# Query norm of a gated-delta attention phase: row sums by one-column matmuls of the squares instead of four transposes and squares with accumulation

## The reference, cut to what matters

```python
q, k, v = silu(conv(mixed))                      # q, k: 16 heads x 128, v: 32 heads x 128
q = inv_scale ** 2 * _rms_norm(q)                # x * rsqrt(mean(x*x) + 1e-6)
k = inv_scale * _rms_norm(k)
# a scan over tokens: state decays, delta = (v - k.state) * beta, state += k x delta, o = q.state
xn = _rms_norm(out) * norm_w
gated = silu(z) * xn
return gated @ W_out
```

## Time and profile before

| | |
|---|---|
| median of 3 runs | 3748.02 us (3746.4 to 3748.84) |
| the profiled execution | 3746.4 us, its span in the trace 3744.6 us |
| TensorE (PE) busy | 3522.7 us, 94% of the span |
| GpSimd (POOL) busy | 2233.1 us, 60% |
| VectorE (DVE) busy | 2110.6 us, 56% |
| ScalarE (ACT) busy | 2081.8 us, 56% |
| granted TensorE clock, mean | 0.976 |

### The profile page before, as it was taken

The page is one execution under the profiler, slowest core; times in us unless marked ns, Lnnn a source line. Parts: engine busy times, 40 slices in busy tenths (PEclk is TensorE's granted clock), DMA queues, the critical chain, the costliest instruction groups (busy, mean ns, idle before and its releaser), DMA issues. The chain is left out here.

```text
span 3744.6 us, 76942 instructions
## 1 busy us (share of the span) xinstructions
PE 3522.7 (94%) x29092; PEld 2941.4 (79%) x29092; DVE 2110.6 (56%) x4091; ACT 2081.8 (56%) x5616; POOL 2233.1 (60%) x2645
## 2 busy tenths in 40 slices
PE   5996599999999999999999999999999999996898
PEld 3884388888888888888888888888888888885787
DVE  4654355555555555555555555555555555552564
ACT  3442266666666666666666666666666666663343
POOL 2101467676767676767676767677777777762110
PEclk8998799999999999999999999999999999997999
DMA  4314112121212121212121212121212121210421
GB/s 152 116 35 83 61 53 74 64 74 64 74 64 74 64 74 64 74 64 75 68 76 64 75 66 80 67 75 64 78 66 80 63 75 67 71 57 35 163 57 35
DMA packets 207871, 270.34 MB, mean 72 GB/s; under 512 B 86160, under 2 KB 117264, under 8 KB 206352
## 3 DMA queue, kind: packets, MB, share of 16 engines
q1 hardware_dynamic: 202464, 250.02, 20.4%
q0 software_dynamic: 4464, 14.36, 1.0%
q10 hardware_dynamic: 576, 1.03, 0.1%
HBM read 176.05 MB, written 89.13 MB: 71 GB/s over the span
## 5 line engine op out<-in xcount | busy, mean ns | idle before, releaser
L1892 ACT ACTIVATE at_t<-at_inv 128x512 f16<-128x512 f32 x768 | 460.2, 599 | 509.2 <-PE at_inv L1701 509.2
L1480 PE MATMUL at_proj<-x_hi,at_w_hi 128*128 128x512 f32 x1024 | 437.6, 427 | 18.0 <-POOL at_w_lo L2151 18.0
L1480 PE MATMUL at_proj<-x_hi,at_w_lo 128*128 128x512 f32 x1024 | 421.5, 412 | 0.0
L1480 PE MATMUL at_proj<-x_lo,at_w_hi 128*128 128x512 f32 x1024 | 415.6, 406 | 0.0
L2230 POOL TENSOR_TENSOR at_gt_lo<-at_cst,at_gates 128x512 fp32r<-128x512 f32 x256 | 261.9, 1044 | 250.2 <-PE at_misc L1480 250.2
L2077 DVE TENSOR_TENSOR at_pml<-at_prod,at_cst 128x256 f16<-128x256 f32 x768 | 322.8, 420 | 147.4 <-PE at_prod L1480 136.5
L2047 DVE TENSOR_TENSOR at_rows<-at_misc,at_rows 128x512 f32<-128x512 f32 x256 | 177.0, 692 | 282.3 <-PE at_misc L1480 281.7
L1480 PE MATMUL at_prod<-at_t,at_nlhi 128*128 128x64 f16 (+1 forms) x3584 | 287.3, 197 | 24.7 <-ACT at_t L1890 13.3
L1480 PE MATMUL at_proj<-at_w_hi,x_hi 128*128 128x256 f32 x1024 | 308.5, 301 | 0.8 <-DVE at_cv_q L2002 0.8
L1480 PE MATMUL at_proj<-at_w_hi,x_lo 128*128 128x256 f32 x1024 | 308.0, 301 | 0.0
L1480 PE MATMUL at_proj<-at_w_lo,x_hi 128*128 128x256 f32 x1024 | 302.3, 295 | 0.0
(11 more groups left out here) (290 smaller groups left out, 10631.3 us busy)
## 6 DMA issues: line engine op xcount, KB each, us to landing
at_rows<-x SPq DMA_DIRECT2D x64, 1024.0 KB, 5.6
x<-at_rows SPq DMA_DIRECT2D x64, 1024.0 KB, 4.2
at_gb<-decays SPq DMA_DIRECT2D x64, 512.0 KB, 3.7
at_raw<-w_qkvz SPq DMA_DIRECT2D x46, 512.0 KB, 3.6
ffn_weights<-ffn_w SPq DMA_DIRECT2D x1, 11776.0 KB, 36.8
ffn_w<-ffn_weights POOLq DMA_DIRECT2D x4, 2688.0 KB, 23.3
at_raw<-w_out SPq DMA_DIRECT2D x16, 512.0 KB, 3.5
f_xnext<-x_in SPq DMA_DIRECT2D x4, 1024.0 KB, 5.2
```

The lines of the kernel that those rows point to most:

```text
L1480: return nc.tensor.matmul(out, lhsT, rhs, start=start, stop=stop)
L1892: own["a_t"].up(A(grown(t16[:, s % R].rearrange("p a t -> p (a t)"), s // R), grown(psT[s % R], s // R), ACT.Copy))
```

## The change

The row sums of the squared q are no longer taken from a transposed q. ScalarE squares the 128x512 `cv_q` in one instruction into `sq[:, 1]`, in step 14 of the first half of the slot. TensorE multiplies each 128x128 chunk of it, as the stationary operand, with one column of ones, which leaves 4 columns of sums in the bank `psT[0]` (`sums`, in `fill[15]`). VectorE scales them and adds epsilon (128x4). GpSimd makes the q factor and its square of it with 3 small instructions. The second norm now multiplies by that square, adds its epsilon, takes the power and multiplies by the q factor: 4 chained instructions in `out_scale` instead of 3. `turn_q` is gone. The projections V0, V1 and K are dealt out anew over `fill[15]` and the gaps; their number stays. TensorE waits for VectorE's read of the sums (`d_ss`) before `turn_v(0)`, which writes the same bank. The waits for `a_sq` in `high`, `kq_of` and `out_scale` go.

```diff
@@ pe_pass
-                def turn_q():
-                    wait(pe, "p_silu", 3 * j + 2)
-                    wait(pe, "a_ex", R * (j + 1))
-                    for c in range(CH):
-                        last = nc.tensor.transpose(ch(psM, c), ch(cv_q, c), ident)
-                    own["s_qtr"].up(last)
+                def sums():
+                    wait(pe, "a_sq", j + 1)
+                    wait(pe, "d_ss", j)
+                    for c in range(CH):
+                        last = mm(psS[:, c:c + 1], ch(sq[:, 1], c), ones[:, 0:1])
+                    own["s_ss"].up(last)
...
-                    fill[15].append(parts(V0_U, 4, 12))
-                    gap[0].append(parts(V1_U, 0, 3))
+                    fill[15] += [parts(V0_U, 4, 9), sums]
+                    gap[0].append(parts(V0_U, 9, 12))
...
-                    gap[5] += [turn_q, parts(V1_U, 8, 10)]
-                    gap[6].append(parts(V1_U, 10, 12))
+                    gap[5].append(parts(V1_U, 5, 9))
+                    gap[6].append(parts(V1_U, 9, 12))
...
-                        gap[9].append(parts(K_U, 8, 12, j + 1))
+                        gap[9].append(parts(K_U, 7, 12, j + 1))
...
                     turn_kn()
+                    wait(pe, "d_ss", j + 1)
@@ act_pass
                 def square_q():
-                    wait(act, "s_qtr", j + 1)
-                    wait(act, "p_fr", j)
-                    for c in range(CH):
-                        last = A(ch(squared, c), ch(psM, c), ACT.Square, scale=(0.25 * Q_EPS / D) ** 0.5, accum_out=qe[:, nxt, c:c + 1])
-                    own["a_sq"].up(last)
+                    wait(act, "p_silu", 3 * j + 2)
+                    wait(act, "s_ss", j)
+                    own["a_sq"].up(A(sq[:, 1, :], conv_out(Q_U), ACT.Square))
...
                     steps[12].append(square_k)
+                    steps[14].append(square_q)
...
                             tanh(V0_U)
-                            square_q()
@@ dve_pass
+                def sums():
+                    wait(dve, "s_ss", j + 1)
+                    wait(dve, "p_rk", 2 * j)
+                    own["d_ss"].up(V.tensor_scalar(ss[:, CH:2 * CH], psS, 0.25 / D, EPS_RMS, ALU.mult, ALU.add))
...
+                if has_prep:
+                    sums()
                 if has_delta:
                     silu_z(Z1_U)
@@ pool_pass, out_scale
-                    chain(G.tensor_tensor(sso[:], sso[:], qe[:, of % 2, :].unsqueeze(1).to_broadcast([P, R, CH]), ALU.add))
-                    chain(G.tensor_scalar(flat, flat, Q_EPS * EPS_RMS, None, ALU.add))
-                    own["p_fr"].up(G.tensor_tensor(fr[:].rearrange("p h c -> p (h c)"), flat, half[:], ALU.pow))
+                    chain(G.tensor_tensor(sso[:], sso[:], qs2[:, of % 2, :].unsqueeze(1).to_broadcast([P, R, CH]), ALU.mult))
+                    chain(G.tensor_scalar(flat, flat, 4 * EPS_RMS, None, ALU.add))
+                    chain(G.tensor_tensor(flat, flat, half[:], ALU.pow))
+                    own["p_fr"].up(G.tensor_tensor(fr[:], sso[:], scale[:, of % 2, CH:2 * CH].unsqueeze(1).to_broadcast([P, R, CH]), ALU.mult))
@@ pool_pass, after mask_g(0)
+                    wait(pool, "d_ss", j + 1)
+                    chain(G.tensor_tensor(rr[:, CH:2 * CH], ss[:, CH:2 * CH], half[:, CH:2 * CH], ALU.pow))
+                    chain(G.tensor_tensor(scale[:, nxt, CH:2 * CH], rr[:, CH:2 * CH], cst[:, C_KSC + CH:C_LATER], ALU.mult))
+                    own["p_rk"].up(G.tensor_tensor(qs2[:, nxt, :], scale[:, nxt, CH:2 * CH], scale[:, nxt, CH:2 * CH], ALU.mult))
```

More of the change, by code:

```diff
@@ L48 @@
 SEGS, WINS = 6, 16
-C_ID, C_INCL, C_KSC = (i * P for i in range(3))
-C_LATER = C_KSC + CH
+C_ID, C_ONES, C_INCL, C_KSC = (i * P for i in range(4))
+C_LATER = C_KSC + 2 * CH
 C_END = C_LATER + P
@@ L285, in constants @@
     c[:, C_LATER:C_LATER + P] = row > col
+    c[:, C_ONES:C_ONES + P] = 1
     c[:, C_INCL:C_INCL + P] = row <= col
     c[:, C_KSC:C_KSC + CH] = INV / 2
+    c[:, C_KSC + CH:C_LATER] = INV * INV / 4
     h = np.zeros((P, C16_END), np.float16)
@@ L1257 @@
 UNITS = NK * B
-Q_EPS = 64 * D * D * EPS_RMS
 def attn_phase(nc, w_qkvz, conv_w, norm_w, w_out, cst_in, cst16_in, x_dram, x_hi, x_lo, gate_dram, decay_dram, y_dram):
@@ L1277, in attn_phase @@
         cst16 = sb("cst16", [P, C16_END], F16)
-        ident, incl = (cst[:, a:a + P] for a in (C_ID, C_INCL))
+        ident, ones, incl = (cst[:, a:a + P] for a in (C_ID, C_ONES, C_INCL))
         ident16, two16 = (cst16[:, a:a + P] for a in (0, C16_TWO))
@@ L1296, in attn_phase @@
         sq = sb("sq", [P, 2, S])
[L1297 to L1300, removed]
+        ss = sb("ss", [P, 2 * CH])
+        rr = sb("rr", [P, 2 * CH])
+        scale = sb("scale", [P, 2, 2 * CH])
+        qs2 = sb("qs2", [P, 2, CH])
         kn = sb("kn", [P, CH, D])
@@ L1321, in attn_phase @@
         ks = sb("ks", [P, R, CH - 1, D])
-        squared = nlhi[:].rearrange("p r s -> p (r s)").bitcast(F32)
         flat = t16[:].rearrange("p r a t -> p (r a t)").bitcast(F32)
@@ L1343, in attn_phase @@
         psO = [psT[1][:, 512:1024], psP[:]]
+        psS = psT[0][:, 768:768 + CH]
         unit_bank = [psA[i] for i in (0, 1, 0, 1, 0, 1)]
@@ L1349, in attn_phase @@
         names = ["l_taps", "l_wo", "l_gates", "l_gb", "l_kq", "l_v", "l_z", "l_x",
-                 "s_proj", "s_z", "s_qtr", "s_ktr", "s_dg", "s_g", "s_kq", "s_p", "s_t", "s_e", "s_t1", "s_v", "s_y", "s_u", "s_o", "s_gtr", "s_w",
+                 "s_proj", "s_z", "s_ss", "s_ktr", "s_dg", "s_g", "s_kq", "s_p", "s_t", "s_e", "s_t1", "s_v", "s_y", "s_u", "s_o", "s_gtr", "s_w",
                  "a_tap", "a_th", "a_thz", "a_ssk", "a_sq", "a_kn", "a_knT", "a_ex", "a_hi", "a_t", "a_t1", "a_v", "a_d", "a_sqo", "a_gt",
-                 "d_conv", "d_silu", "d_z", "d_nl", "d_aqk", "d_p", "d_e", "d_s", "d_gate", "d_lo", "d_y", "d_link",
+                 "d_conv", "d_silu", "d_z", "d_ss", "d_nl", "d_aqk", "d_p", "d_e", "d_s", "d_gate", "d_lo", "d_y", "d_link",
                  "p_w", "p_wo", "p_z", "p_gt", "p_silu", "p_gm", "p_ex", "p_diag", "p_t0", "p_lo", "p_dcy", "p_kg", "p_qg", "p_ks", "p_rk", "p_fr", "p_link"]
         sems = {n: sem(n) for n in names}
-        AHEAD = {"s_proj": 4, "s_qtr": 1, "s_ktr": 2, "s_dg": R, "a_tap": 4, "a_th": 4, "a_ssk": 1, "a_sq": 1, "a_kn": 1, "a_knT": 1, "a_ex": R,
-                 "d_conv": 4, "d_silu": 1, "p_silu": 3, "p_gm": R, "p_ex": R, "p_rk": 1}
+        AHEAD = {"s_proj": 4, "s_ss": 1, "s_ktr": 2, "s_dg": R, "a_tap": 4, "a_th": 4, "a_ssk": 1, "a_sq": 1, "a_kn": 1, "a_knT": 1, "a_ex": R,
+                 "d_conv": 4, "d_silu": 1, "d_ss": 1, "p_silu": 3, "p_gm": R, "p_ex": R, "p_rk": 2}
         def slots():
@@ L1607, in kq_of @@
                 def kq_of(i):
-                    wait(pe, "a_sq", i)
+                    wait(pe, "a_ex", R * i)
                     wait(pe, "p_silu", 3 * i - 1)
@@ L1662, in pe_pass @@
                     fill[14].append(parts(V0_U, 0, 4))
-                    fill[15].append(parts(V0_U, 4, 12))
-                    gap[0].append(parts(V1_U, 0, 3))
+                    fill[15] += [parts(V0_U, 4, 9), sums]
+                    gap[0].append(parts(V0_U, 9, 12))
                     gap[1].append(lambda: gram_of(j + 1))
                     gap[2].append(lambda: decay(0))
-                    gap[3].append(parts(V1_U, 3, 7))
-                    gap[4] += [lambda: decay(1), parts(V1_U, 7, 8)]
-                    gap[5] += [turn_q, parts(V1_U, 8, 10)]
-                    gap[6].append(parts(V1_U, 10, 12))
+                    gap[3].append(parts(V1_U, 0, 4))
+                    gap[4] += [lambda: decay(1), parts(V1_U, 4, 5)]
+                    gap[5].append(parts(V1_U, 5, 9))
+                    gap[6].append(parts(V1_U, 9, 12))
                     gap[10] += [lambda: level_0(j + 1, 0), lambda: kq_of(j + 1)]
                     if j + 2 < UNITS:
-                        gap[6].append(parts(K_U, 0, 2, j + 1))
-                        gap[7].append(parts(K_U, 2, 6, j + 1))
-                        gap[8].append(parts(K_U, 6, 8, j + 1))
-                        gap[9].append(parts(K_U, 8, 12, j + 1))
+                        gap[6].append(parts(K_U, 0, 1, j + 1))
+                        gap[7].append(parts(K_U, 1, 5, j + 1))
+                        gap[8].append(parts(K_U, 5, 7, j + 1))
+                        gap[9].append(parts(K_U, 7, 12, j + 1))
                 if not has_delta:
@@ L1842, in square_q @@
                 def square_q():
-                    wait(act, "s_qtr", j + 1)
-                    wait(act, "p_fr", j)
-                    for c in range(CH):
-                        last = A(ch(squared, c), ch(psM, c), ACT.Square, scale=(0.25 * Q_EPS / D) ** 0.5, accum_out=qe[:, nxt, c:c + 1])
-                    own["a_sq"].up(last)
+                    wait(act, "p_silu", 3 * j + 2)
+                    wait(act, "s_ss", j)
+                    own["a_sq"].up(A(sq[:, 1, :], conv_out(Q_U), ACT.Square))
```

(23 more changed lines are left out.)

## The result

The changed kernel takes 3776.95 us (median of 4 runs, 3776.14 to 3784.43) against 3748.05 us for the kernel before (median of 4 runs). The ratio of the runs is 1.0082 with an interval of 1.0066 to 1.0097: 29 us slower, where 37 were forecast, and inside the forecast range of 3760 to 3808 us. The profiled execution took 3779.27 us.

The account below looks back on a forecast made before the run. The prediction took TensorE's issue stream to bound the kernel. 64 x 0.40 = 25.6 us on TensorE and 63 x 0.18 = 11.3 us from GpSimd make 37 us, giving 3785 us, range 3760 to 3808.

Parts of the forecast that it names:

- What bounds the kernel: Attention phase: TensorE's issue stream sets the slot of 46.25 us; its time counts in full, ScalarE savings for nothing.
- What goes and what comes on TensorE: TensorE's slot: four q transposes (0.43 us) go, eight fp32 loads and one-column moves (0.83 us) come, +0.40 us.
- GpSimd: `out_scale`: the fourth chained instruction, 0.29 us against 0.11 us slack, makes `turn_gated(0)` 0.18 us late a slot.
- the third rival: Existing TensorE waits absorb part of the loss, or GpSimd's step is hidden: 3755 to 3774 us, chance 0.12.
- The new wait of TensorE: Before `turn_v(0)`: the wait for VectorE's read of the sums stays hidden, by 0.2 us.
- What is only moved: `fill[15]` and the gaps: the same 32 projection matmuls keep their time, and gaps covering waits hold at least as much.
- The first rival: `sums` in `fill[15]`: loads hide or are short, 0.03 us a record, giving 3736 or 3747 us; chance 0.11.
- What would show it: Changed kernel's profile: stretch 0.8 to 0.9 us, slot 46.8 us, `turn_gated` waiting some 0.2 us for GpSimd in nearly every slot.

Follow-up runs that it names:

- e2: The changed kernel with 64 columns of ones moved in each of the four sums instead of one; 3783.57 us.
- e3: The changed kernel with squares and ones column in fp16, 4 records with fp16 loads in place of 8 with fp32 loads; 3758.16 us.
- e9: The changed kernel with the dealing of before, fp16 squares, VectorE making the epsilon term and two chained GpSimd instructions in `out_scale`; 3726.73 us.
- e1: The changed kernel with GpSimd's `out_scale` back at three chained instructions (add, add, power) instead of four; 3772.66 us.
- e8: The changed kernel with two more chained 128x8 multiplications by one in `out_scale` on GpSimd; 3811.36 us.
- e6: The kernel before with only the new dealing of the V0, V1 and K projections, `turn_q` staying in `gap[5]`; 3778.63 us.

## Why the prediction was right, and where it was not

- *What bounds the kernel.* Right. What went into TensorE's stream was paid in full, and ScalarE's lighter load bought nothing.
- *What goes and what comes on TensorE.* Right. The one-column records take 0.81 us (0.83 forecast); with `turn_q`'s 0.43 us gone that is +0.38 a slot (+0.40 forecast), 24 of the 29 us. That it is the loads was shown from two sides: 64 columns cost 0.02 us more (e2), the same sums with fp16 loads take 0.12 us (e3, e9). By the Trainium skill ("TensorE: Matmul & The Clock Gate", LDWEIGHTS) a load takes its 128 columns over 1.2 GHz, 107 ns; an estimate from that is 8 loads less `turn_q`, 0.43 us a slot. The trace has 0.116 us between loads, one of them hidden.
- *GpSimd.* The mechanism is right, its size was off: 0.18 us a slot forecast, 0.11 to 0.12 measured (e1, e8 and the offsets). I took the delay of the first load of `turn_gated`, and that came as worked out, 0.17 us. But 0.05 us of it was slack: the four transposes with their loads took 0.54 us from the first load to the next matmul before (1860.31 to 1860.85) and 0.49 after (1832.85 to 1833.34). What holds up the stream is the matmul behind them, 0.12 us late. So the slack was 0.05 us larger than the 0.11 I gave. Over 63 slots this is 4 of the 8 us between 37 and 29. The waits that were there took up nothing (e8), so the third rival is not the reason.
- *The new wait of TensorE.* Right, 0.2 us of cover.
- *What is only moved.* The sum was right, the reason was not. I checked the gaps that gained matmuls and not the place that lost three. There `turn_kn` waits for ScalarE's k; in the kernel before, ScalarE was only some 0.3 us ahead of it. The sums, at 0.81 us, happen to fill the 0.70 us that left. That this term came out at nothing was luck: had they been cheap, the hole would have opened, as in e3.
- *The first rival's price.* Wrong for that reason. I said 3736 to 3747 us if each of the eight records cost 0.03 us, 0.24 us together. e3 has cheaper sums still, 0.12 us, and took 3758.16 us. With 0.24 us, `turn_kn` would have waited for k as well (newton(0), which starts at 1852.13 in the trace of the changed kernel, to `turn_kn` would be 2.48 - 0.81 + 0.24 = 1.91 us, under the 2.05 us that k takes), so e3's time is also the estimate for that case. A forecast of no change would have been 10 us off with the rival's own mechanism granted.
- *What would show it.* The slot and the stretch came as forecast. The row of a wait for GpSimd in every slot did not; it is there only with e8's longer delay.

Not tried: the sums in the reduced fp32 type of the projections, whose matmuls show as one record with one load each. What makes up the 4 us ahead of the first slot in the profiled execution stays open too; the slots explain 30 of 33.

## What to carry to other kernels

To sum over partitions with one column of ones, the data becomes the stationary operand, and its load is the price: here 0.116 us for each of the two records of a 128x128 block in fp32, with 1 column moved and nearly the same with 64, and 0.03 us a block in fp16. These squares only decide how much the second norm's epsilon weighs, so fp16 was open to them. When matmuls are moved on the engine that bounds, look at the place that they leave: what stood behind them had its wait hidden by them.

## What the runs showed that was not expected

Dealing 3 of 32 projection matmuls of a slot to other places cost 0.47 us a slot (e6), as much as a change with real work in it. PE's own row names only 0.26 us of it. The row of its weight loads names more, 0.43 us a slot (530 to 3400 us: total, times, longest):

```profile
PE at_misc L1586 <- ACT at_kn L1862: 16.1, 62, 0.3
PEld at_misc L1586 <- ACT at_kn L1862: 26.9, 62, 0.4
```

The time from newton(1) to `turn_kn` grew by 0.41 us, and the four transposes behind the late load took 0.05 us more. To size a wait of TensorE, read the row of the loads beside that of the matmuls, and take the loss from the distance between starts.
